# One PSUM bank in place of two for the adjacency counts of a graph-attention kernel

## What is computed

```
scores = einsum('ehd,ehd->eh', ft[src], ft[dst]) / sqrt(13)
a      = softmax of scores over the edges of each dst
agg    = segment_sum(ft[src] * a[:, :, None], dst)
...
loops  = arange(n_nodes)
s, d   = concatenate([src, loops]), concatenate([dst, loops])
out    = segment_sum(h[s] * norm[:, None], d) + b
```

## Time and profile before

| | us |
|---|---|
| median of 3 runs | 3872.35 (3868.58 to 3874.59) |
| the profiled execution | 3876.97 |
| its span, first to last instruction | 3875.2 |
| attention: first to last gather | 120.1 to 2077.8 |
| attention: last count, start of its last copy | 1914.38 |

### The profile page before, as it was taken

The page is one execution under the profiler, slowest core; times in us unless marked ns, Lnnn a source line. Parts: engine busy times, 40 slices in busy tenths (PEclk is TensorE's granted clock), DMA queues, the critical chain, the costliest instruction groups (busy, mean ns, idle before and its releaser), DMA issues. The chain is left out here.

```text
span 3875.2 us, 60488 instructions
## 1 busy us (share of the span) xinstructions
PE 3542.1 (91%) x21012; PEld 2105.9 (54%) x21012; DVE 2341.8 (60%) x3454; ACT 1786.6 (46%) x4890; POOL 2357.4 (61%) x2508
## 2 busy tenths in 40 slices
PE   5799999999999999999875888999999999999999
PEld 4566666666666666666654554444544454445444
DVE  8798888888888888888743674222322242214222
ACT  4788888878778878888621464000200020002000
POOL 2577777777777777777774001775277437734772
PEclk7688888888888888888876898999999999999999
DMA  6443334334343343333323215887788678868885
GB/s 203 123 109 105 106 103 107 106 104 106 106 107 103 107 106 103 107 107 107 99 64 78 49 35 163 257 256 223 220 258 256 203 238 258 257 193 261 261 261 176
DMA packets 494657, 599.82 MB, mean 155 GB/s; under 512 B 59929, under 2 KB 426868, under 8 KB 494094
## 3 DMA queue, kind: packets, MB, share of 16 engines
q1 hardware_dynamic: 358950, 341.00, 29.2%
q0 software_dynamic: 79888, 166.31, 17.6%
q10 hardware_dynamic: 55544, 89.04, 6.6%
HBM read 488.04 MB, written 109.69 MB: 154 GB/s over the span
## 5 line engine op out<-in xcount | busy, mean ns | idle before, releaser
L923 POOL DMA_INDIRECT fts<-ft_tab,src_all x1568 | 1481.1, 945 | 477.6 <-issue 477.3
L2296 PE MATMUL cv_acc<-cv_cnt,cv_parts 128*128 128x512 bf16 (+1 forms) x6468 | 1304.7, 364 | 1.0 <-DVE cv_y L2130 1.0
L2296 PEld LDWEIGHTS cv_acc<-cv_cnt,cv_parts 128*128 128x128 bf16 x6468 | 608.3, 98 | 693.4 <-DVE cv_y L2130 1.8
L2069 POOL DMA_INDIRECT cv_slots<-hs_tab,slot_idx x600 | 568.4, 947 | 416.4 <-issue 374.0
L960 DVE TENSOR_TENSOR ohk<-iota_ps,key_cols 128x784 bf16<-128x784 f32 x720 | 665.7, 966 | 5.6
L1212 PE MATMUL agg_ps<-terms,oh 128*64 128x141 f32 x2744 | 544.9, 372 | 35.9 <-DVE terms L997 35.3
L1053 ACT ACTIVATE dist_l<-lo_iota,low 128x128 bf16<-128x128 f16 x1800 | 545.2, 387 | 17.1 <-ACT low L1048 0.7
L1212 PEld LDWEIGHTS agg_ps<-terms,oh 128*64 128x64 f32 x2744 | 472.1, 185 | 90.8 <-DVE terms L997 76.3
L1105 ACT CAST strip<-adj_ps 128x392 bf16<-128x392 f32 x720 | 341.8, 475 | 256.2 <-PE adj_ps L1156 230.1
L974 DVE TENSOR_TENSOR prod<-ftd_ps,fts 128x780 f32<-128x780 f32 (+1 forms) x392 | 271.1, 692 | 285.3 <-DMA fts<-ft_tab,src_all 275.8
L2069 POOL DMA_INDIRECT spare<-hs_tab,slot_idx x296 | 280.2, 947 | 187.4 <-issue 187.4
(11 more groups left out here) (287 smaller groups left out, 3349.8 us busy)
## 6 DMA issues: line engine op xcount, KB each, us to landing
cv_cnt<-adj SPq DMA_DIRECT2D x88, 2048.0 KB, 8.5
cv_cnt<-adj SPq DMA_DIRECT2D x44, 2176.0 KB, 9.6
adj<-strip ACTq DMA_DIRECT2D x180, 392.0 KB
fts<-ft_tab,src_all POOLq DMA_INDIRECT x1568
win<-ft_tab SPq DMA_DIRECT2D x196, 65.0 KB
hs_tab<-cv_hs ACTq DMA_DIRECT2D x24, 448.0 KB, 3.8
cv_slots<-hs_tab,slot_idx POOLq DMA_INDIRECT x600
agg_tab<-res SPq DMA_DIRECT2D x196, 35.2 KB
```

The costliest lines, as they stand in the source:

```text
L923: nc.gpsimd.indirect_dma_start(fts[u][:, k, :], None, ft_tab[:, :], bass.IndirectOffsetOnAxis(src_all[:, n, k:k + 1], 0)).then_inc(gathere ...
L2069: nc.gpsimd.indirect_dma_start(slots[n % RING][:, e, :], None, hs_tab[:, :], bass.IndirectOffsetOnAxis(slot_idx[:, k, at:at + 1], 0)).then ...
L2296: last = nc.tensor.matmul(a[:, 0:width], parts[:, r, b, :], cnt[q][:, 0:width // SUB, (b - b0) * SUB:(b - b0 + 1) * SUB], start=(b == 0 an ...
```

## The change

The two PSUM tiles become one, and `count` waits for the copy of the quarter just before it. The self loops are no longer a product of 392 columns at the head of a quarter that starts the bank; they are a product of 8 columns at its end, of the identity with 8 columns of the identity, into 8 places of the bank (two runs of four). The first of the four counting products starts the bank. The tiles `own` and `own_low`, the four VectorE instructions that fill them and TensorE's wait for these at the head of the stage go. The lists of the engines keep their order.

```diff
-        own = sb("own", [SUB, NA, 2 * KEYS], BF16, c)
-        own_low = sb("own_low", [SUB, 2 * P - SUB], BF16, c)
...
-        adj_ps = [pb(f"adj_ps{q}", [P, 512], F32, c) for q in range(2)]
+        adj_ps = pb("adj_ps", [P, 512], F32, c)
...
-            nc.vector.memset(own[:], 0.0).then_inc(own_made, 1)
-            nc.vector.memset(own_low[:], 0.0).then_inc(own_made, 1)
             nc.vector.memset(hr_3[:], 0.0).then_inc(rest_zero, 1)
-            dve.wait_ge(own_made, 2)
-            nc.vector.tensor_copy(own[:, :, KEYS:KEYS + HALF], ident_bf[0:SUB, 0:SUB].rearrange("p (a d) -> p a d", d=HALF)
-                                  ).then_inc(own_made, 1)
-            nc.vector.tensor_copy(own_low[:, P - SUB:P], ident_bf[0:SUB, 0:SUB]).then_inc(own_made, 1)
...
                 act.wait_ge(adj_done, 4 * k.n + q + 1)
                 nc.scalar.copy(strip[:, k.s, :, QS * q:QS * (q + 1), :].rearrange("p t a d -> p a t d"),
-                               adj_ps[q % 2][:, 0:QS * KEYS].rearrange("p (a t d) -> p a t d", a=QS, d=HALF)
+                               adj_ps[:, 0:QS * KEYS].rearrange("p (a t d) -> p a t d", a=QS, d=HALF)
...
-                if q >= 2 or k.after(1):
-                    pe.wait_ge(strip_done, 4 * k.n + q - 1)
-                tile_of = own[:, q * QS:(q + 1) * QS, KEYS - HALF * k.j:2 * KEYS - HALF * k.j]
-                nc.tensor.matmul(adj_ps[q % 2][:, 0:QS * KEYS], own_low[:, P - SUB - SUB * k.u:2 * P - SUB - SUB * k.u], tile_of, start=True, stop=False)
+                if q or k.after(1):
+                    pe.wait_ge(strip_done, 4 * k.n + q)
+                counts_ps = adj_ps[:, 0:QS * KEYS]
                 for a in range(QS):
                     for m in range(SC):
                         n = q * QC + a * SC + m
-                        last = nc.tensor.matmul(adj_ps[q % 2][:, a * KEYS:(a + 1) * KEYS], ohl[:, k.s, n, :],
-                                                ohk[:, k.s, n, :], start=False, stop=(a == QS - 1 and m == SC - 1))
+                        nc.tensor.matmul(counts_ps[:, a * KEYS:(a + 1) * KEYS], ohl[:, k.s, n, :], ohk[:, k.s, n, :],
+                                         start=(a == 0 and m == 0), stop=False)
+                first = SUB * k.u + q * QS * HALF
+                last = nc.tensor.matmul(counts_ps.rearrange("p (a t d) -> p a t d", a=QS, d=HALF)[:, :, k.j, :], ident_bf[:],
+                                        ident_bf[:, first:first + QS * HALF].rearrange("p (a d) -> p a d", d=HALF),
+                                        start=False, stop=True)
                 last.then_inc(adj_done, 1)
...
-            pe.wait_ge(own_made, 4)
```

More of the change, by code:

```diff
@@ L813, in attention @@
         rest_zero, weights_in = sem("rest_zero"), sem("weights_in")
-        own_made = sem("own_made")
         win_in = [sem(f"win_in{u}") for u in range(UN)]
```

## The result

The changed kernel takes 4216.77 us (median of 4 runs, 4213.82 to 4217.52) against 3873.47 us for the kernel before on the same chip: a ratio of 1.0886, 95% interval 1.0867 to 1.0905, 343 us slower. The profiled execution's span is 4215.8 us.

A forecast was written before the change was run, and what follows sets the result against it. Gathers bound attention at 9.99 us a group; TensorE's ring would then pace at 6.39 + 0.32 + 5.57 = 12.28. 176 x (12.28 - 9.99) - 13 = +390 us, on the median 4262, rounded to 4260 us; range 4050 to 4420.

The forecast's parts named there:

- The gathers' pace before: Attention before the change: GpSimd's gathers pace it at 9.99 us a group; what the change frees on TensorE is worth nothing.
- The way to the sums: TensorE, line 1206 to the sums: 6.39 us in place of 4.25, plus 0.32 for count 3 at 1.2 GHz.
- copy 0 to copy 1: Step on ScalarE's own list within a group: 1.77 us, with count 1 hidden under it.
- the 8 columns: Self-loop product on TensorE: priced at 0.07 us each, bounds from nothing to 0.27.
- Behind the sums: TensorE, from the sums to the next group's line 1206: 5.57 us, where an unhindered group takes 3.75.
- eleven slow groups: Groups in the earlier trace with over 6.3 us to the sums, taken as model: 5.22 to 6.13 us behind them.
- the full-clock ring alone: Rival: full clock throughout, ScalarE's ring of 10.54 us a group sets the pace, 3956 us; chance 0.06.
- The clock itself: TensorE's granted clock in attention: forecast to fall from 0.87 to about 0.75.
- The lead at the end: End of the counted groups: GpSimd is an estimated 1.3 groups ahead, so 13 us come back.
- The waits: Signs: GpSimd waits for `shift`, counts for `strip`, waits for gathered rows nearly gone; line 923 ends near 2470 us.
- today's clock share: Rival: attention's share at 1.2 GHz stays 26%, 11.44 us a group, 4114 us; chance 0.14.
- the gathers still deciding: Rival: ring under 10.06 us, GpSimd's queue hides it, 3872 us as before; chance 0.06.

The follow-up runs named there:

- e1: Changed kernel with two banks in turn as before, self loops still by products of 8 columns: 3874.63 us, ratio 1.0004 to the kernel before.
- e8: Kernel before with five gathers a group in place of eight, so that gathers no longer pace: 3655.19 us, ratio 0.9434.
- e3: Changed kernel plus four idle products of 512 columns ahead of count 2 and again ahead of count 3: 3946.2 us, ratio 1.0193.
- e5: Kernel of e4 plus four idle products of 512 columns ahead of count 2: 3877.87 us, ratio 1.0005.
- e6: Kernel of e1 with quarters 0 and 1 in one bank, 2 and 3 in the other: 3874.63 us, ratio 1.0001.
- e7: Kernel of e1 with quarters 0 and 3 in one bank, 1 and 2 in the other: 3983.39 us, ratio 1.0276.
- e4: Changed kernel with copy 2 and the ten distances ahead of the destination columns, count 3 ahead of closeness: 4062.06 us, ratio 1.0493.
- e9: Kernel of e1 with five gathers a group in place of eight: 3660.12 us, ratio 0.9456.
- e2: Kernel before with one bank, self loops still by the product of 392 columns: 4521.97 us, ratio 1.1678.

## Why the prediction was right

It said 4260 us, 4050 to 4420; 4216.77 was measured. Step by step:

- **The gathers' pace before** The earlier trace rows holds: with two banks nothing that eases TensorE changes the time (e1), and without the pace the old loop is 9.02 us (e8).
- **The way to the sums**: 6.39 + 0.32 = 6.71 us forecast, 6.48 measured. The terms agree with the timeline after: copy 0 to copy 1 1.76 for 1.77, copy 1 to count 2 0.62 for 0.63, copy 2 to count 3 0.63 for 0.63. The surplus is the 8 columns, priced at 0.07 three times: count 2 leads `last_features` by 0.43 us (1009.91 to 1010.34) with them, where 0.44 stood without. They are hidden; the lower end of their bounds was the right one. The 0.27 us that the forecast had by the rule of the Trainium skill, "PSUM — Partial Sum Buffer", section "Specifications (TRN2)", on non-contiguous patterns did not come: the product takes 0.17 us in the trace, behind the counts, and e1 costs nothing. Whether 8 columns in one run would be quicker still, no run shows.
- **Behind the sums**: 5.57 forecast from eleven slow groups, 5.47 measured. That analogy carried the number; the full-clock ring alone would have given 3956, and e3, which has that clock, took 3946. The clock itself was put at 0.75 and was 0.79. That the two means are only 0.10 us apart is partly luck: the eleven groups run from 5.22 to 6.13 us, while after the change 5.98 and 4.96 us take turns (the latter from 1013.06 to 1018.02), and no part of the forecast led one to expect the turns. (The forecast counts 149 groups between 348 and 1790 us; the trace has 144 there, the same eleven among them.)
- **The lead at the end**: 13 us were taken off; 345 us by the group's length against 341 in the span leave about 4.
- **The waits** came as said: GpSimd on `shift`, counts on `strip`, none on gathered rows to speak of. The last gather came at 2417 us in place of 2470, since the group is shorter than forecast.
- **The rivals**: today's clock share (4114) was the nearest below, and lost because the share at 1.2 GHz rose from 26% to 42%, with the stalls now in every group; the gathers still deciding fails by 2 us a group. The kernel of the Trainium skill's page "TensorE: Matmul & The Clock Gate", section "HAM oscillation — how this bites in real kernels", gained nothing more from a second PSUM buffer; here the second bank is worth 342 us (e1 against the changed kernel). e5 shows where both can hold: with another order and the wait filled, one bank is enough.

The forecast rise was 390 us against 341 in the span, 49 too many: 0.23 us a group to the sums make 40, 0.10 behind them 18, and the lead gives back about 9.

## What to carry to other kernels

Before a buffer is taken away, write down the ring that its hand-overs close over both engines' lists, everything between two uses included, and compare it with what paces the loop now: e6 waits 235 us for nothing, e7 closes the ring and pays. Add the clock: price the work behind a stall at the slow groups that the trace already has, not at the fast ones (here 5.57 us for a measured 5.47, where the fast group has 3.75). Where a wait must stay, the order of the lists and idle products in it are two ways out: each alone leaves a part of the loss (e4 189 us, e3 73), both together none (e5).

## What was not expected of the hardware

- Idle products make the kernel faster: 271 us in e3, with a clock of 0.99 in place of 0.79.
- With two banks the clock is lower without the 392-column products: 0.84 for 0.87 (e1 against the kernel before) and 0.87 for 0.95 (e9 against e8). With one bank it is the other way round: 0.79 for 0.69 (the changed kernel against e2). What the lower clock costs with two banks isn't shown: the gathers hide it in e1, and VectorE leaves no room in e9.
- One long stall a group, 1.24 us, goes with a clock of 0.77 in e4, no higher than with two (0.79); one of 1.16 us goes with 0.86 in e6. So the length of a stall alone does not tell the clock, and what does stays open.
